# Early tiles half a batch sooner, and half of the random features formed at the end of the second read

## The reference

```python
x = x + _L1_xattn_ref(_layernorm(x), ctx_1024, ctx_1024, ...)   # 16 heads read the context
x = x + _L1_attn_ref(_layernorm(x), input_weights, xis, proj_matrix)
x = x + _L1_ffn_ref(_layernorm(x), ...)                         # three trees of 16 leaves, then attention

# _L1_attn_ref: ab = xis, AB = exp(xis), gs = proj_matrix
def _rfs(xw, ab, AB, gs):
    dot_products = jnp.einsum('...d,rd->...r', xw, ab[:, None] * gs)
    correction = (0.5 * jnp.sum(xw * xw, axis=-1))[..., None] * (ab * ab)
    return 1.0 / math.sqrt(NUM_RFS) * AB * jnp.exp(dot_products - correction)
weights = _rfs(input_weights, ab, AB, gs)
feats = _rfs(x, ab, AB, gs)
return jnp.einsum('bsr,or->bso', feats, weights)
```

## Time and profile before

| what | value |
|---|---|
| median of 3 runs | 1489.73 us (1486.0 to 1492.95) |
| the profiled execution, its own time | 1487.85 us |
| its span | 1486.0 us |
| granted TensorE clock, mean | 0.945 |
| PE busy | 1352.8 us (91%) |
| DVE busy | 1007.3 us (68%) |
| ACT busy | 649.7 us (44%) |
| POOL busy | 693.7 us (47%) |
| last half of the last batch begins, span time | 1223.3 us |
| the tail's first VectorE instruction | 1268.12 us |
| first tree product (L2758) | 1317.84 us |

### The profile page before, as it was taken

The page is one execution under the profiler, slowest core; times in us unless marked ns, Lnnn a source line. Parts: engine busy times, 40 slices in busy tenths (PEclk is TensorE's granted clock), DMA queues, the critical chain, the costliest instruction groups (busy, mean ns, idle before and its releaser), DMA issues. The chain is left out here.

```text
span 1486.0 us, 29141 instructions
## 1 busy us (share of the span) xinstructions
PE 1352.8 (91%) x11182; PEld 1096.0 (74%) x11182; DVE 1007.3 (68%) x2023; ACT 649.7 (44%) x1223; POOL 693.7 (47%) x589
## 2 busy tenths in 40 slices
PE   7899768589879999999999999999999997789998
PEld 4556455479857888888888888888888865457787
DVE  6998743545655777787778778777776656364444
ACT  3556213310063655555555555555555432433322
POOL 0242001120245677976697678766886433412200
PEclk9999978779988999999999999999999966799999
DMA  9998135007155777787779777977684540220000
GB/s 359 416 380 317 57 138 190 1 0 248 67 148 167 208 194 184 211 220 194 183 201 230 195 177 203 230 194 181 177 202 108 127 112 8 89 114 0 1 1 29
DMA packets 107575, 240.11 MB, mean 162 GB/s; under 512 B 30218, under 2 KB 76634, under 8 KB 104746
## 3 DMA queue, kind: packets, MB, share of 16 engines
q1 hardware_dynamic: 89070, 216.75, 51.4%
q10 hardware_dynamic: 18368, 21.50, 4.2%
HBM read 152.96 MB, written 6.40 MB: 107 GB/s over the span
## 5 line engine op out<-in xcount | busy, mean ns | idle before, releaser
L2337 DVE TENSOR_REDUCE d_top<-psum 128x1 f32<-128x400 f32 (+2 forms) x512 | 285.7, 574 | 82.6 <-PE psum L1939 74.2
L1850 POOL TENSOR_TENSOR d_ring<-d_ring 128x512 f32<-128x512 f32 x224 | 287.2, 1282 | 67.0 <-ACT d_ring L2153 49.2
L2153 ACT ACTIVATE d_ring<-psum 128x512 f32<-128x512 f32 (+1 forms) x416 | 230.1, 595 | 166.6 <-PE psum L1957 127.4
L1957 PEld LDWEIGHTS psum<-d_queries,d_stack 100*128 100x128 f32 (+1 forms) x1664 | 212.0, 194 | 41.0 <-issue 25.5
L1957 PE MATMUL psum<-d_queries,d_stack 100*128 100x128 f32 (+1 forms) x1664 | 231.2, 281 | 8.9 <-DVE d_queries L2352 5.9
L1939 PE MATMUL psum<-d_stack,d_queries 96*128 96x400 f32 (+1 forms) x512 | 204.0, 402 | 6.6 <-DVE d_top L2337 5.5
L1923 PE MATMUL psum<-d_wv,d_rowsT 128*128 128x256 f32 (+1 forms) x1248 | 208.1, 284 | 0.0
L1923 PEld LDWEIGHTS psum<-d_wv,d_rowsT 128*128 128x128 f32 (+1 forms) x1248 | 194.1, 187 | 2.0 <-issue 0.5
L1787 POOL TENSOR_TENSOR d_rowsT<-shared,d_rowsT 128x768 fp32r<-128x768 f32 (+2 forms) x62 | 118.5, 1913 | 154.7 <-ACT d_rowsT L2124 154.7
L1913 PE MATMUL psum<-d_rowsT,d_wk 128*128 128x384 f32 (+2 forms) x768 | 159.2, 357 | 10.4 <-DVE d_bv L2470 7.3
L1913 PEld LDWEIGHTS psum<-d_rowsT,d_wk 128*128 128x128 f32 x768 | 133.7, 193 | 21.9 <-DVE d_bv L2470 7.4
(11 more groups left out here) (415 smaller groups left out, 2170.9 us busy)
## 6 DMA issues: line engine op xcount, KB each, us to landing
d_stack<-d_stage SPq DMA_DIRECT2D x384, 200.2 KB, 4.3
a_cT<-ctxT_dram SPq DMA_DIRECT2D x14, 1601.0 KB, 13.7
a_cR<-ctx_rows_dram ACTq DMA_DIRECT2D x12, 1664.0 KB, 10.9
shared<-moe_w_dram SPq DMA_DIRECT2D x16, 1024.0 KB, 10.2
shared<-row_stds_dram SPq DMA_DIRECT2D x16, 801.0 KB, 6.6
shared<-ctxT_dram SPq DMA_DIRECT2D x32, 384.0 KB, 6.4
shared<-ctx_rows_dram SPq DMA_DIRECT2D x12, 896.0 KB, 6.0
shared<-ctx_rows_dram SPq DMA_DIRECT2D x12, 768.0 KB, 5.7
```

Of the source, the lines that this page charges most:

```text
L1850: pool.tensor_tensor(sums[:, 0, m, :], first, ring[:, slot_of(u, m, c), :], ALU.add)\
L1957: last = pe.matmul(ps[0:w, S_BANK + (m + c) % 2, j * P:(j + 1) * P], stack[0:STACKED, m, j, c * P:c * P + w], queries[0:STACKED, m, j, :], ...
L2153: act.activation(ring[0:w, slot_of(u, m, c), :], ps[0:w, S_BANK + (m + c) % 2, :], ACT.Exp)\
L2337: dve.tensor_reduce(top[:, m, v:v + 1], ps[:, M_BANK + v % 2, 0:min(w, S - s0)], X, ALU.max)\
```

## The change

Positions in the last batch are now pairs (half, group). The EARLY tiles' moments stand at (0, 5) where they stood at (1, 1), the roots at (0, 6) for (1, 2), normalising at (1, 0) for (1, 3), transposes at (1, 1) for (1, 4), copies at (1, 2) for (1, 5), projection at (1, 3) for (1, 6). The seven tiles' sums into `x` move from behind the loop into it, at (1, 4). New in the loop are, for the first four tiles (HEAD), the moments of the next layernorm at (1, 5), and at (1, 6) their roots, the squared norms and the normalised rows. A squared norm is now D times variance times the square of the root's inverse; it enters the exponent as a diagonal matrix (`diagonals`: the identity scaled per token by ScalarE) in one product with `half`, in place of two products with squares. GpSimd forms `gw`, `half` and the weights' squares at (0, 6), from the pack `pe`, which SP now loads in front of the EARLY tiles' return. Behind the loop TensorE transposes the four HEAD tiles, forms the weights' and the four tiles' exponents, before and after `turn_tokens(LATE)` and before the LATE tile's transposes.

The tail is left with the other four tiles, and it starts with the product of the four finished ones. All roots are now Ln and Exp. The order is rewritten so that the trees' layernorm of tiles 0 to 3 stands ahead of the second product; the `b2` and `member` copies move to the end of ScalarE's part, and three of four splits of the first tree's weights stand behind the second set of features. Many of the tail's buffers now lie in the tile `shared` of the phases before.

The diff, cut to its core:

```diff
--- before.py
+++ after.py
...
+def exponent(pe, bank, gw, half, m, rhs, square):
+
+    for k in range(KD):
+        pe.matmul(bank, gw[:, k, m * P:(m + 1) * P], rhs[:, k], start=(k == 0), stop=False)
+    return pe.matmul(bank, half[:, m * P:(m + 1) * P], square, start=False, stop=True)
+
+
+def roots_of(act, sig, tag, scratch, eps, tiles, v):
+
+    _, moments, _, std, rstd = scratch
+    act.activation(std[:, tiles], moments[:, tiles, 1], ACT.Ln, bias=eps).then_inc(sig(f"{tag}_ln"), 1)
+    act.wait_ge(sig(f"{tag}_ln"), v)
+    act.activation(rstd[:, tiles], std[:, tiles], ACT.Exp, scale=-0.5).then_inc(sig(f"{tag}_rstd"), 1)
+
+
+def squared_norms(dve, sig, tag, scratch, norm, tiles):
+
+    _, moments, _, _, rstd = scratch
+    dve.tensor_tensor(norm[:, tiles], moments[:, tiles, 1], rstd[:, tiles], ALU.mult).then_inc(sig(f"{tag}_norm"), 1)
+    dve.wait_ge(sig(f"{tag}_norm"), 1)
+    dve.scalar_tensor_tensor(norm[:, tiles], norm[:, tiles], float(D), rstd[:, tiles], ALU.mult, ALU.mult)\
...
-        STATS_AT, ROOTS_AT, NORM_AT, TURN_AT, TAKE_AT, PROJECT_AT = 1, 2, 3, 4, 5, 6
+        STATS_AT, ROOTS_AT, NORM_AT, TURN_AT, TAKE_AT, PROJECT_AT = (0, 5), (0, 6), (1, 0), (1, 1), (1, 2), (1, 3)
+        ADD_AT, MEASURE_AT, SPREAD_AT, FEATURES_AT = (1, 4), (1, 5), (1, 6), (0, 6)
+        HEAD = 4
...
+            sp.wait_ge(sig("d_scaled"), 4 * (B - 1))
+            sp.dma_start(core.packs["pe"], drams["pe"]).then_inc(sig("d_pe_in"), 16)
...
+                        if b == B - 1 and (m, g) == FEATURES_AT:
+                            feature_weights()
...
+                for k in range(KD):
+                    pool.tensor_tensor(gw[:, k, :], core.w("rf_gsT")[:, k, :], core.p("rf_ab"), ALU.mult).then_inc(sig("h_gw"), 1)
+                pool.tensor_tensor(half, core.p("rf_ab"), core.p("rf_ab"), ALU.mult).then_inc(sig("h_absq"), 1)
+                pool.wait_ge(sig("h_absq"), 1)
+                pool.tensor_scalar(half, half, -0.5, None, ALU.mult).then_inc(sig("h_half"), 1)
...
+                    pool.tensor_tensor(wsq[k], core.w("rf_iwT")[:, k, :], core.w("rf_iwT")[:, k, :], ALU.mult)\
+                        .then_inc(sig("h_wsq"), 1)
+                pool.wait_ge(sig("h_wsq"), KD)
+                pool.tensor_tensor(wsq[0], wsq[0], wsq[1], ALU.add).then_inc(sig("h_wsqT"), 1)
...
+            def weight_exponent(m):
+
+                exponent(pe, ps[:, S_BANK + m, 0:D], shared.gw, shared.half, m, core.w("rf_iwT"), shared.wsq[0])\
+                    .then_inc(sig("h_wexp_ps"), 1)
+
+            pe.wait_ge(sig("h_ln_out"), HEAD)
+            pe.wait_ge(sig("d_sum"), EARLY // 2 + 1)
+            for k in range(KD):
+                for t in range(HEAD):
+                    last = pe.transpose(ps[:, F_BANK + k, t * P:(t + 1) * P], feature_rows[:, t, k * P:(k + 1) * P],
+                                        core.p("ident"))
+                last.then_inc(sig("h_xnT_ps"), 1)
+            pe.wait_ge(sig("h_gw"), KD)
+            pe.wait_ge(sig("h_half"), 1)
+            pe.wait_ge(sig("h_wsqT"), 1)
+            wait(pe, "d_exp", NC * QUADS)
+            weight_exponent(0)
             turn_tokens(LATE)
+            weight_exponent(1)
+            for s, v in both(sig, "h_xnT", 1):
+                pe.wait_ge(s, v)
+            pe.wait_ge(sig("h_spread"), HEAD)
+            for m in range(KD):
+                exponent(pe, ps[:, M_BANK + m, :], shared.gw, shared.half, m, feature_xT, diagonals).then_inc(sig("h_exp_ps"), 1)
             pe.wait_ge(sig("d_ln2_out"), NT)
+            pe.wait_ge(sig("h_wfeats"), KD)
             for k in range(KD):
                 last = pe.transpose(ps[:, S_BANK + k, 0:P], nat2(LATE)[:, k * P:(k + 1) * P], core.p("ident"))
...
+                        if b == B - 1 and (m, g) == SPREAD_AT:
+                            act.wait_ge(sig("h_moments"), HEAD)
+                            roots_of(act, sig, "h", feature_scratch, eps[:, 0:1], slice(0, HEAD), 1)
...
+            act.wait_ge(sig("h_norm"), 2)
+            act.wait_ge(sig("d_x"), EARLY // 2 + 1)
+            for t in range(HEAD):
+                act.activation(diagonals[:, t, :], core.p("ident"), ACT.Copy, scale=norm[:, t:t + 1])\
...
+            weight_features(0)
             take_tokens(LATE)
+            weight_features(1)
+            features(0)
             roots(slice(LATE, NT), 2)
+            features(1)
             take_rows((LATE,), ps[:, S_BANK, 0:P], len(TURNS) + 1)
...
+            def close(at):
+
+                if at == STATS_AT:
+                    moments_of(dve, sig, "d_ln2", scratch3, res, range(EARLY), [(sig("d_early_in"), 16)])
...
+                elif at == ADD_AT:
+                    dve.wait_ge(sig("d_early_biased"), 1)
+                    for i in range(EARLY // 2):
+                        add_tiles(i)
+                    add_tile(EARLY - 1, 1)
+                elif at == MEASURE_AT:
+                    moments_of(dve, sig, "h", feature_scratch, x, range(HEAD), [(sig("d_x"), HEAD // 2)])
+                elif at == SPREAD_AT:
+                    dve.wait_ge(sig("h_rstd"), 1)
+                    squared_norms(dve, sig, "h", feature_scratch, norm, slice(0, HEAD))
+                    _, moments, _, _, rstd = feature_scratch
+                    for t in range(HEAD):
+                        dve.tensor_scalar(feature_rows[:, t, :], x[:, t, :], moments[:, t, 0:1], rstd[:, t:t + 1],
+                                          ALU.subtract, ALU.mult).then_inc(sig("h_ln_out"), 1)
...
-            add_tile(EARLY - 1, 1)
+            dve.wait_ge(sig("h_xnT_ps"), 2)
+            dve.tensor_copy(feature_xT[:, 1, :], ps[:, F_BANK + 1, :]).then_inc(sig("h_xnT_d"), 1)
...
+        raw = shared.trees
...
+            def add_features(c):
+
...
+                            last = pe.matmul(ps[:, i, j * D:(j + 1) * D], feats[c][:, k, (t % 4) * P:(t % 4 + 1) * P],
+                                             wfeats[:, k, :], start=(k == 0), stop=(k == KD - 1))
...
+            def turn_rows(c, bank, done, tag):
+
+                pe.wait_ge(sig(f"{tag}_ln_out"), done)
...
+            add_features(0)
+            turn_rows(1, 2, NT // 2, "e")
+            for sm, n in both(sig, "e_xnT", 1):
+                pe.wait_ge(sm, n)
+            pe.wait_ge(sig("e_spread"), NT // 2)
+            for m in range(KD):
+                exponent(pe, ps[:, 6 + m, :], gw, half, m, xnT[:, :, cols_of(1)], spread[:, :, :]).then_inc(sig("e_exp_ps"), 1)
+            turn_rows(0, 4, NT // 2, "f")
+            pe.wait_ge(sig("e_feats"), KD)
+            add_features(1)
+            pe.wait_ge(sig("f_params_in"), 16)
+            nodes(0)
+            turn_rows(1, 6, NT, "f")
+            nodes(1)
...
+            act.wait_ge(sig("e_eps"), 1)
+            act.wait_ge(sig("e_ln_moments"), NT // 2)
+            roots_of(act, sig, "e_ln", scratch, eps[:, 0:1], REST, 1)
+            act.wait_ge(sig("e_norm"), 2)
+            for t in range(NT // 2):
+                act.activation(spread[:, t, :], core.p("ident"), ACT.Copy, scale=norm[:, NT // 2 + t:NT // 2 + t + 1])\
+                   .then_inc(sig("e_spread"), 1)
...
-            features(0)
-            features(1)
...
-            split_weights(0, 0)
-            split_weights(0, 1)
-            features(2)
-            split_weights(0, 2)
-            split_weights(0, 3)
-            features(3)
-            for j in range(TREES):
-                act.activation(member[:, j, :], leaf_raw[:, j, :], ACT.Copy).then_inc(sig("f_member"), 1)
-            for c in range(2):
...
+            def f_roots(c):
+
...
+            def f_turned(c):
+
...
+            f_roots(0)
+            split_weights(0, 0)
+            features(0)
+            features(1)
+            f_turned(0)
+            for q in range(1, 4):
+                split_weights(0, q)
+            f_roots(1)
+            f_turned(1)
+            act.wait_ge(sig("f_leaf_in"), 32 * TREES)
+            act.activation(b2[0][:, :], b2_raw[:, :], ACT.Copy).then_inc(sig("f_b2H"), 1)
+            for j in range(TREES):
+                act.activation(member[:, j, :], leaf_raw[:, j, :], ACT.Copy).then_inc(sig("f_member"), 1)
...
+            moments_of(dve, sig, "e_ln", scratch, x, range(NT // 2, NT), base=NT // 2)
+            dve.wait_ge(sig("e_ln_rstd"), 1)
+            squared_norms(dve, sig, "e", scratch, norm, REST)
+            normalise("e_ln", scratch, range(NT // 2, NT))
+            for i in range(2):
+                add_out(i)
+            dve.wait_ge(sig("e_xnT_ps"), 2)
+            dve.tensor_copy(xnT[:, 1, cols_of(1)], ps[:, 3, :]).then_inc(sig("e_xnT_d"), 1)
+            for i in range(2):
+                measure(i)
+            dve.wait_ge(sig("f_ln_rstd"), 1)
+            normalise("f_ln", scratch2, range(NT // 2))
+            turned(0)
+            lows(0)
+            for i in range(2, 4):
+                add_out(i)
+                measure(i)
+            dve.wait_ge(sig("f_ln_rstd"), 2)
```

(5 more changed lines are left out.)

## The result

The changed kernel takes **1476.3 us** (median of 6 runs, 1468.6 to 1477.8) against 1490.9 us for the kernel before on the same chip (6 runs): a ratio of 0.989, 95% interval 0.987 to 0.991. On two further chips it took 1477.4 and 1476.2 us (6 runs each; ratios 0.992 [0.989, 0.995] and 0.989 [0.986, 0.991]). The prediction was 1476.9.

What follows compares the result with a forecast made beforehand. TensorE was taken to bound the last half at its low clock, a chain of waits the tail. 3.5 - 16.4 = -12.9 us on 1487.85 gives 1475.0; the median's 1.9 more makes 1476.9, range 1472 to 1481.

Steps and rivals of the forecast that it cites:

- Term 1: End of the second read: projection sooner, but VectorE's added work delays denominators and token; phase ends 3.5 us later.
- Seven take 2.4: Normalising seven EARLY tiles at (1, 0), with GpSimd idle, takes VectorE 2.4 us instead of 7.52.
- VectorE's 10.7 us hang behind it: Behind the projection, VectorE's sums, moments, sums of exponentials and rows take 10.7 us, to 1254.2, before the denominators.
- The token at 1259.5, 4.5 later: ScalarE's copy of the LATE token, behind transposes, one weight exponent and an exponential, comes at 1259.5, 4.5 us later.
- They fit by 1 us: Second weight exponent and twelve passes before the LATE transposes fit beside some 7.4 us of round trip, by 1 us.
- Term 2: The tail from its start to the first tree product: 33.3 us against 49.7, 16.4 us sooner.
- over 1 us each: In the tail, normalising of tiles 4 to 7 beside GpSimd's pieces takes over 1 us per tile.
- Both end together: At the tail's end, TensorE's leaves (33.3 us from its start) and ScalarE's `member` copies (32.7) end together.
- A: Rival: TensorE's clock stays low until after the projection, which ends 8.5 us later; kernel takes 1485; chance 0.08.
- B: Rival: low level lasts through the token exponents of read and tail; 10 us slower than before, 1499.5; chance 0.04.
- C: Rival: the loop's gain stays and GpSimd's pieces miss the rows; read +2, tail 20 us sooner: 1471; chance 0.11.
- D: Rival: transfers (`pe` before the EARLY return, first tree before the features) are the new wait, 3 to 5 us: 1480; chance 0.07.

Runs made afterwards that it cites:

- the third execution: The changed kernel itself, unaltered, run once more beside other kernels for comparison on the same chip: 1476.2 us.
- the first experiment: The kernel before with only the EARLY tiles' six steps, moments to projection, half a batch sooner: 1490.4 us, ratio 0.9991.
- the run with the three orders: The changed kernel with sums split, weight exponents and diagonals earlier, first tree's transfer first and ScalarE's tail reordered: 1469.4 us, ratio to before 0.987.
- the split sums: The changed kernel with only tiles 0 to 3 summed inside the loop, tiles 4 to 6 behind the last heads: 1475.0 us, ratio to before 0.989.
- the early transfer: The changed kernel with the first tree's transfer issued first in the tail, every engine's order kept: 1477.1 us.

## Why the prediction was right

Its time was right (1476.9 against 1476.3) and so was the mechanism; some sizes were off, in both directions. That it came within 1 us is luck: the forecast was a gain of 12.9 us, the three pairs of medians show 14.6, 13.5 and 15.7, and the start it was counted from, the median of three runs, lies 1.2 us below that of six.

*Term 1, forecast +3.5, measured +2.5 (+4.6 in the third execution).* "TensorE loses 1.25 us" at the first denominators: their start moved from 2.3 to 3.5 us behind the mark, 1.2. "Seven take 2.4": 2.34. "The projection ends at 1243.5", 7 us sooner: it ended 19.5 us behind the mark instead of 27.3, 7.8 sooner. "VectorE's 10.7 us hang behind it": 1239.57 to 1250.41, 10.8. "The token at 1259.5, 4.5 later": 3.7 later, because the level rose again at the weight exponent ahead of it (1.4 us, where I had allowed 1.3 to 2.6). The chain behind the token was 10.6 us against 11.7. "They fit by 1 us": the LATE transposes waited 1.25 us for VectorE. The step that was half wrong is the one behind the sum: it had the gain of the earlier steps given back by the features' chain, while the first experiment shows that even without that chain only 1.25 us of the projection's gain reached the end of the read: most of it was groups that had changed sides with the projection.

*Term 2, forecast 33.3 us, measured 31.97.* Rows ready at T + 4.8 (4.5), product to T + 5.2 (5.3), exponents to T + 12.3 (12.4). Then three sizes failed, two of them against each other. The tree's split began at T + 13.8, not 12.6: its issue stood at T + 6.0, but it landed only some 7.7 us later, at a point where I had taken off the time of the pack `pe`. The second product took 5.41 us, not 3.5: I had TensorE idle ahead of the features, and did not ask at which level it would come out of 2.84 us of idleness. So VectorE was done at T + 23.2, not 21.1. Against that, four rows were normalised in 1.75 us, not 4.4: only the last 0.6 us of GpSimd's last piece lay beside them, since the pieces were shorter and VectorE later. So "over 1 us each" was not seen. How these two play into each other shows in the third execution, where TensorE waited 1.43 us and the second product took 3.73, VectorE came sooner and met more of the pieces:

```profile
1298.73 3.10 DVE L3074 TENSOR_SCALAR shared<-x,f_ln_moments,f_ln_rstd 128x256 f32<-128x256 f32 x4 [0.60 <-ACT f_ln_rstd L1579]
```

The stretch was 31.65 all the same. The last part, "transposes 1.7, nodes 3.46, leaves", 7.2 us, took 6.5. "Both end together": member at 1299.08, the leaves' pass at 1299.11.

The Trainium skill, "SBUF — State Buffer", section "SBUF: two separate sides", has the shared pair of ports locked for a whole instruction. The traces agree in kind: the last piece ended at 1291.85, and the four rows begun at 1291.22 took 1.75 us, 0.36 more than the tail's other four (1.39) for an overlap of 0.63; and in the run with the three orders two operations of 0.65 us took 2.42 each beside pieces of 2.08. What failed in my sum was not the rule but when the two would meet.

*The trees, "168 us".* 167.4 to 167.7 in the changed kernel. Between kernels and executions this part varies from 167.4 to 169.9, mostly by whether TensorE enters it at the low level (four profiles, 169.1 to 169.6).

*The rivals.* A is refuted for this order by the trace; its price of 8.5 us was not measured, only its two groups (2.6 us, as forecast). B did not happen; its sum should have given 1499.7, not 1499.5. C, the loop's gain stays, was wrong at its root, as above. D was half true: the transfer did gate the features, and removing it was worth nothing until VectorE and ScalarE were put in order behind it.

What I had not seen is where the gain comes from. The prediction priced the tail as a whole. By parts, about 11 of its 17.7 us are the weights' features, the fewer passes, the roots without table loads and the normalising without GpSimd beside it, of which only the diagonal was tried by itself (1.3 us), and the move of the features, which gives the change its name, nets 1.6 to 3.3. Whether it gains anything is open: 1.5 us between medians of six runs is less than they can tell.

## What to carry to other kernels

Before you take a wait away, name what ends next on every engine at that point: of four single alterations here (the earlier steps, the diagonal, the split sums, the early transfer) none could be told from nothing by its median, and the last two, taken together with their neighbours mended, were worth 9 on top of the change. Place VectorE's subtractions and scalings that read only SBUF where GpSimd is idle, and its reads of PSUM beside it. When a profile is luckier than the runs, measure from a mark that stands ahead of the change.

## What the runs showed of the hardware

TensorE's level did not follow its busy share: scores and weighings at 4.00 of 4.00 us busy left it at 1.2 GHz for 10 us and more, and with 14 transposes in the same place it was at 2.4 GHz 6 to 8 us behind the last wait (ten profiles). In the kernel with the diagonal alone 14 transposes behind a wait of 2.75 us did not lift it, and later it was at 0.57 for 4 us in the midst of the trees. A wait of 2.84 us ahead of the tail's second product was followed by 5.41 us for 16 passes, one of 1.43 (the changed kernel's third profile) by 3.73.

Beside GpSimd's subtractions, some of VectorE's operations on SBUF alone stretch whatever their size: a scaling of four columns took 1.38 instead of 0.17 us (beside 80x768), a subtraction of 128x512 2.42 instead of 0.65 (beside 128x1024). In the changed kernel's tail, beside pieces of 128x1024, its sums out of PSUM took 0.69 us, and its moments, which read SBUF alone, 0.75 for two tiles, as they did with GpSimd idle (0.74).
